# Both projection chunks at the head of a head pair's TensorE work, the value chunks spread one to a head pair

## The reference

```python
h = _ln(x, ln1_g, ln1_b) + shift
qkv = (h @ Wqkv.T).reshape(b, n, 3, H, HD)
q = _ln(qkv[:, :, 0].transpose(0, 2, 1, 3), qn_g, qn_b)
k = _ln(qkv[:, :, 1].transpose(0, 2, 1, 3), kn_g, kn_b)
v = qkv[:, :, 2].transpose(0, 2, 1, 3)
attn = jax.nn.softmax(jnp.einsum('bhnd,bhmd->bhnm', q, k) / jnp.sqrt(jnp.float32(HD)), axis=-1)
o = jnp.einsum('bhnm,bhmd->bhnd', attn, v).transpose(0, 2, 1, 3).reshape(b, n, H * HD)
x = x + o @ Wout.T
gate = jax.nn.softmax(x.reshape(-1, d) @ Wgate.T, axis=-1)   # then top_k, the experts, scatter-add
```

## Time and profile before

| what | us |
|---|---|
| median of 3 runs | 1293.33 |
| lowest and highest of them | 1288.46, 1294.29 |
| the profiled execution | 1290.78 |
| its span, first to last instruction | 1288.8 |

### The profile page before, as it was taken

How to read it: one execution, slowest core, us unless ns; L and a number is a source line. 1 busy time by engine, 2 the same in 40 slices (tenths; PEclk the granted TensorE clock), 3 DMA queues, 4 the chain that set the end, 5 groups by cost and what they waited for, 6 DMA issues and landing times.

```text
span 1288.8 us, 24533 instructions
## 1 busy us (share of the span) xinstructions
PE 1107.9 (86%) x8291; PEld 855.0 (66%) x8291; DVE 1043.5 (81%) x1956; ACT 626.6 (49%) x1002; POOL 565.6 (44%) x507
## 2 busy tenths in 40 slices
PE   4689999999999999999999999999975046999996
PEld 3457676767767676767767676767753044888886
DVE  8688988888898988888898988888886863767773
ACT  4445555556465556555464655555441003544531
POOL 3465544444454544444453544454451202345342
PEclk9799999999999999999999999999998556999999
DMA  4000000000101000000001000000003121355322
GB/s 171 9 1 18 18 18 17 16 16 16 33 0 33 16 16 16 16 16 16 27 5 33 16 16 16 16 16 16 9 25 136 42 74 35 99 160 132 102 38 29
DMA packets 32277, 48.50 MB, mean 38 GB/s; under 512 B 7920, under 2 KB 28528, under 8 KB 30960
## 3 DMA queue, kind: packets, MB, share of 16 engines
q1 hardware_dynamic: 26096, 39.49, 9.4%
q0 software_dynamic: 6144, 8.52, 3.7%
HBM read 35.29 MB, written 12.71 MB: 37 GB/s over the span
## 4 chain that ended last, share of the span: by engine, by line
PE 62%; DVE 22%; issue 8%; POOL 4%; ACT 2%; DMA 2%; DVEq 0%; ACTq 0%; POOLq 0%
PE ch L444 10%; PE ch L446 9%; PE ch L445 9%; PE av L1270 7%; PE sc L1295 7%; DVE rec L1123 4%; PE sc L1286 4%; PE av L1274 3%; PE pq L1248 3%; DVE qn L807 3%; POOL out L541 2%; PE mx L1306 2%; DVE var L1165 2%; POOL got L529 1%; DVE hit L694 1%
## 5 line engine op out<-in xcount | busy, mean ns | idle before, releaser
L899 POOL TENSOR_TENSOR qk_lo<-qkT,qk_hi 128x512 fp32r<-128x512 f32 x128 | 165.3, 1291 | 272.8 <-ACT qk_hi L965 272.8
L1123 DVE RECIPROCAL rec<-av 128x256 f32<-128x256 f32 x128 | 224.5, 1754 | 45.6 <-PE av L1274 45.0
L977 ACT ACTIVATE prob<-sc 128x1024 f32<-128x1024 f32 x128 | 131.4, 1027 | 236.6 <-PE sc L1295 236.6
L894 POOL TENSOR_TENSOR prob_sum<-prob 128x512 f32<-128x512 f32 x128 | 165.1, 1290 | 140.6 <-ACT prob L977 140.6
L444 PE MATMUL ch<-w_hi,hT_lo 128*128 128x512 f32 x384 | 174.1, 453 | 6.6 <-DVE w_lo L1045 6.5
L1270 PE MATMUL av<-prob,V 128*64 128x256 f32 x1024 | 141.0, 396 | 43.6 <-DVE oT L1125 41.6
L1145 DVE TENSOR_REDUCE m<-mx 128x4 bf16<-128x1024 f32 x128 | 155.4, 1214 | 0.0
L445 PE MATMUL ch<-w_lo,hT_hi 128*128 128x512 f32 x384 | 153.9, 401 | 0.0
L446 PE MATMUL ch<-w_hi,hT_hi 128*128 128x512 f32 x384 | 153.0, 398 | 0.0
L1270 PEld LDWEIGHTS av<-prob,V 128*64 128x64 f32 x1024 | 65.7, 137 | 101.4 <-issue 81.3
L1081 DVE TENSOR_REDUCE ssum<-sq 128x8 f32<-128x512 f32 x128 | 84.8, 680 | 55.3 <-ACT sq L944 53.5
(11 more groups left out here) (189 smaller groups left out, 2752.0 us busy)
## 6 DMA issues: line engine op xcount, KB each, us to landing
fcw<-experts SPq DMA_DIRECT2D x8, 2048.0 KB, 9.0
x_sb<-x SPq DMA_DIRECT2D x16, 256.0 KB, 2.8
xr_sb<-x SPq DMA_DIRECT2D x16, 256.0 KB, 2.7
out<-tok SPq DMA_DIRECT2D x16, 256.0 KB, 2.2
rows_dram<-xh SPq DMA_DIRECT2D x16, 256.0 KB, 2.2
prob<-w_qkvT SPq DMA_DIRECT2D x2, 512.0 KB, 7.1
qn<-w_qkvT SPq DMA_DIRECT2D x2, 512.0 KB, 7.8
V<-w_qkvT SPq DMA_DIRECT2D x2, 512.0 KB, 7.6
```

Of the source, the lines that this page charges most:

```text
L894: nc.gpsimd.tensor_tensor(prob_sum[(hp - 1) % 2][:, :, :], pr[:, :, 0, :], pr[:, :, 1, :], ALU.add).then_inc(prob_summed, 1)
L899: nc.gpsimd.tensor_tensor(qk_lo[par][:, :], qkT[par][:, :], qk_hi[par][:, :].bitcast(F32), ALU.subtract).then_inc(lo_ready, 1)
L977: nc.scalar.activation(prob[hp % 2][:, :], sc[:, :], ACT.Exp, scale=HD ** -0.5).then_inc(prob_ready, 1)
L1123: chain(nc.vector.reciprocal(rec[:, :], av[:, N:2 * N]))
```

## The change

In every pass TensorE now does both chunks first, then the transposes, values, scores and pre-score. The second v chunk of each half moves from passes 1 and 5 to passes 2 and 6, so that no pass holds two of them. In pass 6 the token transposes and the gate's product become positions 1 and 2 of the bank order. ScalarE takes the chunks' raw copies ahead of `qkT`, and the second square after `qk_hi`. VectorE takes the first head sum ahead of the reciprocal, and the copy of the logits behind the maxima. In pass 2 VectorE waits for the v chunk of that pass before it overwrites `hT_hi`, and pass 2 then reads the old one.

```diff
-CHUNKS = {(7, 0): ("q", 0), (7, 1): ("k", 0), (0, 0): ("q", 1), (0, 1): ("k", 1), (1, 0): ("v", 0), (1, 1): ("v", 1),
-          (3, 0): ("q", 0), (3, 1): ("k", 0), (4, 0): ("q", 1), (4, 1): ("k", 1), (5, 0): ("v", 0), (5, 1): ("v", 1)}
-ODD_STEPS = (0, 1, 7)
+CHUNKS = {(7, 0): ("q", 0), (7, 1): ("k", 0), (0, 0): ("q", 1), (0, 1): ("k", 1), (1, 0): ("v", 0), (2, 0): ("v", 1),
+          (3, 0): ("q", 0), (3, 1): ("k", 0), (4, 0): ("q", 1), (4, 1): ("k", 1), (5, 0): ("v", 0), (6, 0): ("v", 1)}
+ODD_STEPS = (0, 1, 2, 7)
...
-        out += [(0, 2, "wout", "dve"), (6, 0, "tokT", "act"), (6, 1, "gate", "dve")]
+        out += [(0, 2, "wout", "dve"), (6, 1, "tokT", "act"), (6, 2, "gate", "dve")]
... (ScalarE, a pass)
+                    if 0 in live:
+                        chunk(b, hp, 0, "raw")
+                        chunk(b, hp, 0, "square")
+                    if 1 in live:
+                        chunk(b, hp, 1, "raw")
                     if ahead:
...
                         nc.scalar.activation(qk_hi[par][:, :], qkT[par][:, :], ACT.Copy).then_inc(hi_ready, 1)
-                    if live:
-                        chunk(b, hp, 0)
+                    if 1 in live:
+                        chunk(b, hp, 1, "square")
... (VectorE, a pass)
                         need(act_read, through("act", b, (1, 2)))
+                        if cur:
+                            need(slot_filled, through("slot", b, (2, 0)))
                         chain(nc.vector.tensor_copy(hT_hi[:, :, :], hT[:, :, :]))
...
+                    if hp in (0, 3, 4, 7) and (cur if hp < 2 else nxt):
+                        head_sums(b, hp, 0)
                     if (cur and hp > 0) or (hp == 0 and prv):
...
                     if hp in (0, 3, 4, 7) and (cur if hp < 2 else nxt):
-                        head_sums(b, hp, 0)
                         head_sums(b, hp, 1)
-                    if hp == 6 and prv:
-                        need(slot_filled, through("slot", b, (6, 1)))
...
                         nc.vector.tensor_reduce(m[(hp + 1) % 2][:, :], mx[:, :].rearrange("p (a j) -> p a j", a=4),
                                                 AX.X, ALU.max).then_inc(max_ready, 1)
+                    if hp == 6 and prv:
+                        need(slot_filled, through("slot", b, (6, 2)))
+                        nc.vector.tensor_copy(dst, ch[slot_bank(b, (6, 2))][:, 0:TT * E]).then_inc(dve_read, 1)
... (TensorE, a pass)
+                    for pos in live:
+                        chunk(b, hp, pos)
                     if ahead:
...
-                    if live:
-                        chunk(b, hp, 0)
...
-                    if live:
-                        chunk(b, hp, 1)
```

More of the change, by code:

```diff
@@ L69, in batch_slots @@
     cur, nxt, prv = 0 <= b < B, b + 1 < B, 1 <= b <= B
-    out = [(hp, pos, name, "act") for (hp, pos), (name, _) in CHUNKS.items() if (cur if hp < 2 else nxt)]
+    out = [(hp, pos, name, "act") for (hp, pos), (name, _) in CHUNKS.items() if (cur if hp < 3 else nxt)]
     if prv:
-        out += [(0, 2, "wout", "dve"), (6, 0, "tokT", "act"), (6, 1, "gate", "dve")]
+        out += [(0, 2, "wout", "dve"), (6, 1, "tokT", "act"), (6, 2, "gate", "dve")]
     if nxt:
@@ L930, in weights_high, with chunk @@
                         nc.scalar.activation(w_hi[:, c, 2 * H * HD:], raw_v(c), ACT.Copy).then_inc(wv_hi_ready, 1)
-            def chunk(b, hp, pos):
+            def chunk(b, hp, pos, part):
                 key = (hp, pos)
@@ L935, in chunk @@
                 name, t = CHUNKS[key]
+                if name == "v" and part == "square":
+                    return
                 g = group_of(b, hp)
@@ L941, in chunk @@
                     need(qn_ready if c >= POOL_CHUNKS else qn_pool_ready, g)
-                    nc.scalar.activation(raw[:, c, :], bank[:, :], ACT.Copy)
-                    need(chunk_summed, through("chunk", b, key) - 2)
-                    nc.scalar.activation(sq[c % 2][:, :], bank[:, :], ACT.Square).then_inc(act_read, 1)
+                    if part == "raw":
+                        nc.scalar.activation(raw[:, c, :], bank[:, :], ACT.Copy)
+                    else:
+                        need(chunk_summed, through("chunk", b, key) - 2)
+                        nc.scalar.activation(sq[c % 2][:, :], bank[:, :], ACT.Square).then_inc(act_read, 1)
                 else:
@@ L953, in batch @@
                     ahead = (cur and nxt) or (cur and hp < UNITS - 1) or (nxt and hp == UNITS - 1)
-                    live = (hp, 0) in CHUNKS and (cur if hp < 2 else nxt)
+                    live = [pos for pos in range(2) if (hp, pos) in CHUNKS and (cur if hp < 3 else nxt)]
+                    if isinstance(b, int) and b < 0 and hp in (2, 5):
+                        weights_high(0 if hp == 2 else 1)
+                    if 0 in live:
[3 more added lines that the diff above has]
+                        chunk(b, hp, 1, "raw")
                     if ahead:
@@ L1212, in chunk @@
                 if pos == 0:
-                    need(hT_split, b + 1 if hp < 2 else b + 2)
+                    need(hT_split, b + 1 if hp < 3 else b + 2)
                 if isinstance(b, int) and b < 0 and pos == 0:
@@ L1315, in batch @@
                     if hp == 6 and prv:
-                        bank = take_bank(b, (6, 1))
-                        need(act_read, through("act", b, (6, 0)))
+                        bank = take_bank(b, (6, 2))
+                        need(act_read, through("act", b, (6, 1)))
                         for t in range(TT):
```

17 lines of the change are left out of this document (6 added, 11 removed).

## The result

| | before | after |
|---|---|---|
| median of 4 runs each, same chip | 1293.24 us (1288.46 to 1294.29) | 1333.03 us (1328.46 to 1334.23) |
| ratio | | 1.0303, interval 1.0284 to 1.0322 |
| span of the profiled execution | 1288.8 | 1332.3 |
| one undisturbed batch of the loop | 58.20 | 60.62 |
| VectorE's waits for the squares | 53.5 in 37 | 9.1 in 16 |

The kernel is 3% slower. The page of after answers to the earlier trace rows, the list of waits to the earlier trace rows (columns: who waits, for whom, total us, count, longest one).

The account below looks back on a forecast made before the run. Neither engine alone bounds it: TensorE (86% busy) and VectorE (81%) take turns waiting. 1290.8 + 28 (batches, +2.1 each) + 4 (clock) - 5 (start) = 1318 us; range 1288 to 1342.

Parts of the forecast that it names:

- (a): Pass 4: head sums no longer wait for the squares, so VectorE's stretch shrinks by 1.94 us, to 19.2.
- (b): Pass 3: TensorE's 0.52 us wait before the scores goes; 0.6 us a batch gained, with small change elsewhere.
- (c): Start: pass 7's two chunks fill TensorE's 9.30 us idle, Newton chain of batch 0 comes earlier; 5 us gained once.
- The bank: Pass 7: second chunk waits about 2.5 us for VectorE to empty the logits' bank; +1.6 us a batch.
- `hT_lo`: Pass 2: VectorE's `hT_lo` meets GpSimd's `qk_lo`, delaying the first chunk of pass 3; +1.1 us a batch, ends 0 and 1.9.
- the clock: TensorE's granted clock falls behind long waits: 4 more drops at 1.4 us, +4 us in all, ends -1 and +14.
- The Newton chain: VectorE's small steps after V4: stalls as long as before, one meeting with GpSimd replaced by another; stretch 19.2 us.
- the first rival: Newton chain starts in a GpSimd gap, `hT_lo` slips past: -0.5 us a batch, 1274 to 1279 us; chance 0.18.

Follow-up runs that it names:

- a_v_together: Changed kernel with both v chunks of a half together in passes 1 and 5 again, VectorE's pass 2 without the v-chunk wait: 1382.0 us, ratio 1.0714.
- b_logit_late: Kernel before the change with only the copy of the gate's logits moved behind the maxima of pass 6: 1288.5 us, ratio 0.9966.

## Why the prediction was right, and where it was not

It gave 1318 with 1288 to 1342, slower; 1333.0 was measured. The mechanism that it put first is the one that happened, at the place that it named. By its own steps:

- **(a), the gain on VectorE.** Right. The waits for the squares went from 53.5 to 9.1 us.
- **(b), the scores of pass 3.** Right. The 0.52 is gone, V3 to V4 is 0.60 shorter.
- **(c), the start.** 5 us taken, 3.4 measured, inside its ends. One execution of each sizes it badly: V1 of batch 1 comes at 109.2 to 115.3 in the ten kernels with the changed order and at 117.8 to 119.1 in the three with the old one. So the gain is there, and 3.4 is near its small end.
- **The bank.** Idle 2.5 foretold, 2.35 measured; V4 to V7 22.8 foretold, 22.62 measured. Undoing it gave 2.57 a batch. The sizes are right, by +1.6 against +1.45.
- **`hT_lo`.** 1.1 foretold, 0.82 measured. It took 1.66 instead of 0.69 in the earlier trace rows since `qk_lo` began 0.24 us ahead of it:

```profile
368.04 1.35 POOL L899 TENSOR_TENSOR qk_lo<-qkT,qk_hi 128x512 fp32r<-128x512 f32 x1 [1.93 <-ACT qk_hi L976]
```

```profile
368.28 1.66 DVE L1113 TENSOR_TENSOR hT_lo<-hT,hT_hi 128x512 fp32r<-128x512 f32 x1
```

- **The step that failed: a wait not seen.** The prediction says that what moves on TensorE is who waits, and then prices the passes 2 to 7 and the start; of pass 0 it says nothing. The output projection there begins when GpSimd has made `o_lo` of pair 6. Before, that was there 1.64 us ahead of the projection (341.17 + 0.74 = 341.91, against 343.55):

```profile
339.94 1.27 POOL L899 TENSOR_TENSOR qk_lo<-qkT,qk_hi 128x512 fp32r<-128x512 f32 x1 [2.17 <-ACT qk_hi L965]
341.17 0.74 POOL L904 TENSOR_TENSOR o_lo<-oT,o_hi 128x256 fp32r<-128x256 f32 x1
```

```profile
343.55 0.28 PE L444 MATMUL ch<-wo_hi,o_lo 128*128 128x256 f32 x1
```

and after:

```profile
411.24 1.29 POOL L899 TENSOR_TENSOR qk_lo<-qkT,qk_hi 128x512 fp32r<-128x512 f32 x1 [3.06 <-ACT qk_hi L976]
412.48 0.73 POOL L904 TENSOR_TENSOR o_lo<-oT,o_hi 128x256 fp32r<-128x256 f32 x1
```

Two moves use the 1.64 up. The chunk (0, 1), 1.51 us, no longer stands between the pre-score and the projection. And the transposes, from which `qkT`, `qk_hi`, `qk_lo` and then `o_lo` follow, start 0.53 us ahead of V0 instead of 1.96, so `qk_lo` starts 1.98 after V0 instead of 1.04. By these rows, as an estimate, either alone would have left next to no wait; both together leave 0.89. That is 0.9 x 14 = 12.6 us, and the reason why the loop's undisturbed part was +34 and not the +28 of the sum (the smaller terms for the bank and `hT_lo`, together some -6, hide the other half). The order of after shows the place, had it been asked for each reader of a slow engine what now stands ahead of it, and what ahead of the instruction that starts that engine's work.
- **The term that was mis-sized: the clock.** 4 more drops, +4 us in all, were taken; the net was 5 more, and 9.5 us. A drop costs 1.56, not 1.4, and none of it is hidden by VectorE, since the chunk that is slowed stands behind the bank. Its upper end, 14, had room for it.
- **The Newton chain.** "Stalls as long as before" came out (4.34 us instead of 4.45) and by the way that it described: the first two steps lie ahead of GpSimd and later ones under it. VectorE and GpSimd of after, at the chain of that batch:

```profile
385.84 0.17 DVE L1175 TENSOR_SCALAR var<-ssum 128x32 f32<-128x32 f32 x1
386.04 0.17 DVE L1177 TENSOR_SCALAR var<-mv 128x2 f32<-128x2 f32 x1
...
387.46 1.18 DVE L1009 SCALAR_TENSOR_TENSOR na<-ny 128x36 f32<-128x36 f32 x1
388.68 0.67 DVE L1010 TENSOR_TENSOR na<-na,var 128x36 f32<-128x36 f32 x1
```

```profile
387.30 1.29 POOL L899 TENSOR_TENSOR qk_lo<-qkT,qk_hi 128x512 fp32r<-128x512 f32 x1 [1.84 <-ACT qk_hi L976]
388.55 0.74 POOL L904 TENSOR_TENSOR o_lo<-oT,o_hi 128x256 fp32r<-128x256 f32 x1
```

But one sentence there does not hold: "No row shows these small ones stalled". The trace of the kernel before has such a row. The group of that line over the whole span (shortest, median and longest in ns) tells of it:

```profile
L1002 DVE SCALAR_TENSOR_TENSOR na<-ny x105: 194/196/1291, 5.3 to 1053.8; 128x36 f32<-128x36 f32 x54, 128x34 f32<-128x34 f32 x51
```

It stands in the last batch, with GpSimd's sum of the exponentials beside it:

```profile
959.03 1.29 DVE L1002 SCALAR_TENSOR_TENSOR na<-ny 128x36 f32<-128x36 f32 x1
```

```profile
959.01 1.26 POOL L894 TENSOR_TENSOR prob_sum<-prob 128x512 f32<-128x512 f32 x1 [0.98 <-ACT prob L977]
```

With 1291 beside 194 in sight, the first rival (VectorE gets clear of GpSimd) deserved less than its 0.18: for it to win, a chain that starts early must not be caught further down. The rule of the Trainium skill, "SBUF — State Buffer", section "SBUF: two separate sides", that a VectorE instruction with two SBUF inputs and a GpSimd one that reads SBUF keep each other out for whole instructions, says the same. The trace agrees: 1.18 for 0.20 us, with its end at 388.64, behind that of `qk_lo` at 388.59.
- **The range.** It held, with 9 us to its upper end. The middle was 15 us low. Of the profiled executions' 43.4 us, 27 were forecast; the missing 16 are 12.6 from `o_lo`, less some 7 for the bank, `hT_lo` and the rest of a batch, some 5.5 of clock, 1.6 at the start and 3.4 behind V1 of the last batch. That the sizes of the bank and of `hT_lo` erred the other way, and so hid half of the wait not seen, was luck.

## What to carry to other kernels

When instructions of an in-order engine change places, list for each consumer of a slower engine (bank, operand, split) what stood between it and the instruction that started that engine's work, and what stands there now: both the expected wait and the missed one were of this kind. Where one engine waits once for a stretch of another, move the release out of that stretch (here: the gate's product and its copy) before undoing the new order: that and three more moves of the same kind of small step turned 3% slower into 2.7% faster. And a gain of under a microsecond a batch can vanish in the clock of TensorE: read the granted clock before a repair is called useless.

## What the runs showed of the hardware

- **GpSimd's work holds up the smallest VectorE operations too.** The 128x36 steps with two SBUF operands, 0.20 us alone, took 1.18 and 0.67 under GpSimd's `qk_lo` and `o_lo`; the profile shows this as a long duration and not as idle time, so no list of waits has it. The single-input `hT_hi` (CAST, 128x512) is 0.42 us in the batch shown of after, where it starts 0.21 ahead of `qk_lo`, and was 1.50 in a_v_together, where `qk_lo` (446.53, 1.76) had begun 0.55 ahead of it.
- **Holes of 2.2 to 2.4 us are enough for the clock to fall, but not always.** They did in 2 of 14 batches before (58.20 us long), 7 of 14 after (60.62, every second), 14 of 14 with the early split (its batch 59.77 without the drop), and in none where 1.24 or, with the useless products, 0.7 was left at the logits. The hole alone does not decide: the early split takes another wait out of the batch, leaves this hole as it is, and doubled the drops; b_logit_late (batch 57.98) keeps the hole of 2.2 before V6 that before has, and shows none. No run tells what rule decides it.
- **Useless work can pay.** 98 products, 24.8 us of TensorE's time, in a hole that was idle anyway, made the loop's batches 10.6 us shorter in all.
